# DLRM tower on one core: dense matmuls, stores and the last steps of the tail put in another order

## The reference

```python
e = jnp.stack([tbl_f[ids[:, f]] for f in range(39)], axis=1)      # (512, 39, 16)
xk, outs = e, []
for W in (W0, W1):
    Wr = W.reshape(39, xk.shape[1], 128)
    xk = jnp.einsum('bid,bjd,ijh->bhd', e, xk, Wr)
    outs.append(xk)
z = jnp.sum(jnp.concatenate(outs, axis=1), axis=-1)               # (512, 256)
h = jnp.concatenate([z, dense_ctx], axis=1)                       # (512, 272)
h = jnp.maximum(h @ W_top1 + b_top1, 0.0)                         # (512, 512)
h = jnp.maximum(h @ W_top2 + b_top2, 0.0)                         # (512, 256)
y = h @ W_top3                                                    # (512, 1)
```

## Time and profile before

| what | value |
|---|---|
| median of 3 runs | 257.5 us |
| lowest and highest of them | 256.31 and 258.46 us |
| the profiled execution's own time | 257.7 us |
| its span (first to last instruction) | 255.9 us |
| PE, DVE, POOL, ACT busy | 211.4, 180.1, 157.0, 149.3 us |
| mean granted clock of PE | 0.946 |

### The profile page before, as it was taken

How to read it: one execution, slowest core, us unless ns; L and a number is a source line. 1 busy time by engine, 2 the same in 40 slices (tenths; PEclk the granted TensorE clock), 3 DMA queues, 4 the chain that set the end, 5 groups by cost and what they waited for, 6 DMA issues and landing times.

```text
span 255.9 us, 3948 instructions
## 1 busy us (share of the span) xinstructions
PE 211.4 (83%) x1212; PEld 165.7 (65%) x1212; DVE 180.1 (70%) x335; ACT 149.3 (58%) x284; POOL 157.0 (61%) x165
## 2 busy tenths in 40 slices
PE   0458294971989898999898979997989799998996
PEld 0223153750766586888575868885768688876995
DVE  1497595944899979796979696969796968841000
ACT  2134254670778766776687566776876566866002
POOL 4777777777677777777777777777777750000000
PEclk9999859597699999999999999999999799999799
DMA  6200032295411202020202020202020201010000
GB/s 193 68 6 6 7 52 69 39 280 135 108 20 20 31 10 33 9 33 8 32 9 33 9 31 6 32 9 33 8 32 9 32 9 19 6 27 4 0 3 0
DMA packets 27511, 9.40 MB, mean 37 GB/s; under 512 B 22513, under 2 KB 25585, under 8 KB 27490
## 3 DMA queue, kind: packets, MB, share of 16 engines
q1 hardware_dynamic: 22370, 7.86, 13.7%
q0 software_dynamic: 5120, 1.29, 5.3%
HBM read 6.50 MB, written 0.00 MB: 25 GB/s over the span
## 4 chain that ended last, share of the span: by engine, by line
PE 42%; POOL 26%; issue 12%; DMA 9%; DVE 8%; ACT 2%; DVEq 0%; ACTq 0%; POOLq 0%
POOL gathered L348 26%; PE tower L671 10%; DMA gathered<-table,rows 8%; PE copies L622 7%; PE sums L636 4%; PE sums L637 4%; PE sums L638 4%; PE ring L660 3%; PE ring L661 2%; PE ring L662 2%; DVE turned L408 2%; DVE parts L399 1%; ACT dots L532 1%; DVE columns L442 1%; PE ring L650 1%
## 5 line engine op out<-in xcount | busy, mean ns | idle before, releaser
L348 POOL DMA_INDIRECT gathered<-table,rows x160 | 156.6, 979 | 51.7 <-issue 44.2
L428 DVE TENSOR_TENSOR prod_lo<-prod,prod_hi 128x512 fp32r<-128x512 f32 x96 | 65.0, 690 | 3.3 <-ACT prod_hi L498 3.3
L622 PE MATMUL copies<-turned,sel_sb 128*128 128x512 bf16 x112 | 42.7, 434 | 28.9 <-DVE turned L408 28.6
L420 DVE TENSOR_TENSOR prod<-first,copies 128x512 f32<-128x512 f32 x96 | 64.0, 681 | 2.8 <-ACT first L489 1.3
L498 ACT CAST prod_hi<-prod 128x512 fp32r<-128x512 f32 x96 | 58.2, 625 | 9.1 <-DVE prod L420 9.1
L671 PEld LDWEIGHTS tower<-dots,w_sb 128*128 128x128 f32 x312 | 47.7, 199 | 5.0 <-issue 0.8
L671 PE MATMUL tower<-dots,w_sb 128*128 128x128 f32 x312 | 49.8, 284 | 0.3 <-ACT dots L532 0.2
L532 ACT COPY dots<-ring 128x320 f32<-128x320 f32 x64 | 43.6, 746 | 8.0 <-PE ring L662 6.9
L636 PE MATMUL sums<-prod_hi,w_hi 128*128 128x512 f32 x96 | 47.6, 496 | 0.4 <-DVE prod_lo L428 0.2
L637 PE MATMUL sums<-prod_lo,w_hi 128*128 128x512 f32 x96 | 38.8, 404 | 0.0
L622 PEld LDWEIGHTS copies<-turned,sel_sb 128*128 128x128 bf16 x112 | 10.3, 103 | 44.0 <-DVE turned L408 33.8
(11 more groups left out here) (85 smaller groups left out, 237.8 us busy)
## 6 DMA issues: line engine op xcount, KB each, us to landing
gathered<-table,rows POOLq DMA_INDIRECT x160
diag<-columns SPq DMA_DIRECT2D x128, 20.0 KB
wt_sb<-wt SPq DMA_DIRECT2D x2, 512.0 KB
sel_f<-sel SPq DMA_DIRECT2D x1, 448.0 KB, 3.0
w0a<-w_ij SPq DMA_DIRECT2D x1, 448.0 KB, 4.4
w0b<-w_ji SPq DMA_DIRECT2D x1, 448.0 KB, 5.4
ids_sb<-ids SPq DMA_DIRECT2D x1, 85.0 KB, 2.0
ident_f<-ident SPq DMA_DIRECT2D x1, 64.0 KB, 2.8
```

Of the source, the lines that this page charges most:

```text
L348: pool.indirect_dma_start(gathered[0:n, k % NGATHER, q, :], None, table, bass.IndirectOffsetOnAxis(ap=rows[0:n, k, q:q + 1], axis=0)).then ...
L420: nc.vector.tensor_tensor(prod[:, m % NPROD, :], first[:, k % 2, :], copies[n % 3][:], ALU.mult)\
L428: nc.vector.tensor_tensor(prod_lo[:, m % NPART, :], prod[:, m % NPROD, :], prod_hi[:, m % NPART, :], ALU.subtract).then_inc(lo_ready, 1)
L622: pe.matmul(copies[n % 3][:], sel_sb[:, e, :], turned[:, k % NTURN, :], start=True, stop=True).then_inc(copied, 1)
```

## The change

1. A new step `last_dense` in PE's order, right ahead of `x1` of block 15: the four 16-row matmuls of the dense features of group 3 (what L701 did), one into each h1 bank.
2. Of the last block's four dot stores ACT keeps 0 and 2; DVE takes 1 and 3, after its last low part.
3. Tower step 3 of group 2 (PE's L693) is moved from between the last dots to behind layer 2, and ACT's two relus of step 2 from ahead of the last dot stores to behind them.
4. Layer 2 of group 3 starts right after the last dot stores. Its bank is `sums[1]` in place of `tower`; `tower` becomes the first h2 bank. The four z1 matmuls (what L700 did) and tower step 3 of group 2 follow it.
5. DVE takes two of the four h1 relus (1 and 3).

No DMA is added or moved.

```diff
--- before.py
+++ after.py
@@ -124,8 +124,8 @@
 
 GROUP_TENSOR = (dict(layer2=6.22, rate=2.58, tower=(23.18, 26.7, 31.41)),
                 dict(layer2=6.11, rate=2.84, tower=(24.45, 27.61, 30.02)),
-                dict(layer2=6.49, rate=2.72, tower=(22.71, 30.79, 31.9)))
-GROUP_SCALAR = ((23.33, 26.23, 29.15, 32.32), (22.1, 26.57, 28.3, 32.76), (21.63, 26.88, 32.35, 75.59))
+                dict(layer2=6.49, rate=2.72, tower=(22.71, 30.79)))
+GROUP_SCALAR = ((23.33, 26.23, 29.15, 32.32), (22.1, 26.57, 28.3, 32.76), (21.63, 26.88, 34.6))
 GROUP_VECTOR = (23.59, 23.68, 25.09)
 
 
@@ -140,7 +140,8 @@
                 if isinstance(steps, float):
                     items.append((STEPS * k + steps, (name, k)))
                 else:
-                    items.extend((STEPS * k + step, (name, k, n)) for n, step in enumerate(steps))
+                    items.extend((STEPS * k + step, (name, k, n)) for n, step in enumerate(steps)
+                                 if items is not act or (name, k) != ("dot", BLOCKS - 1) or n % 2 == 0)
     for g in range(GROUPS - 1):
         end = STEPS * (GROUP // BLOCK) * (g + 1)
         when = group_tensor[g]
@@ -148,6 +149,7 @@
         pe.extend((end + step, ("tower", g, n + 1)) for n, step in enumerate(when["tower"]))
         act.extend((end + step, ("tower", g, n)) for n, step in enumerate(group_scalar[g]))
         dve.append((end + group_vector[g], ("h1", g)))
+    pe.append((STEPS * (BLOCKS - 1) + tensor["x1"] - 0.01, ("last_dense",)))
     return [[what for _, what in sorted(items, key=lambda x: x[0])] for items in (pe, act, dve)]
 
 
@@ -224,7 +226,8 @@
         dense_banks = [*sums, tower, sums[0]]
 
         h1_banks = [*copies, sums[0]]
-        h2_banks = [sums[1], ring[0]]
+        z2_bank = sums[1]
+        h2_banks = [tower, ring[0]]
         y_bank = ring[1]
 
 
@@ -269,8 +272,11 @@
         tower_drained = sem("tower_drained")
         h1_summed = sem("h1_summed")
 
+        last_dots = sem("last_dots")
+        last_z2_full = sem("last_z2_full")
+        last_z2 = sem("last_z2")
         last_h1_full = sem("last_h1_full")
-        last_h1 = sem("last_h1")
+        last_h1 = [sem(f"last_h1_{n}") for n in range(H1 // P)]
         last_h2_full = sem("last_h2_full")
         last_h2 = [sem(f"last_h2_{n}") for n in range(H2 // P)]
         last_y_full = sem("last_y_full")
@@ -286,6 +292,13 @@
 
         def by_sub(of):
             return of[:, 0:SUBS * WIDE].rearrange("p (s i) -> p s i", i=WIDE)
+
+        def dots_at(k, s):
+            g, at = divmod(k * BLOCK + s * SUB, GROUP)
+            return dots[:, g % 2, :, at:at + SUB].rearrange("p i b -> p b i")
+
+        def dots_of(n):
+            return ring[n % 2][:, 0:SUB * WIDE].rearrange("p (b i) -> p b i", i=WIDE)
 
         block = ctx.enter_context(nc.Block())
 
@@ -463,7 +476,15 @@
                 {"split": split, "columns": columns_low, "product": product, "low": low,
                  "squares": square_low, "x1": turned_low, "h1": h1_sum}[what[0]](*what[1:])
 
+            for s in range(1, SUBS, 2):
+                n = ring_no["dot", BLOCKS - 1, s]
+                dve.wait_ge(ring_full, n + 1)
+                nc.vector.tensor_copy(dots_at(BLOCKS - 1, s), dots_of(n)).then_inc(last_dots, 1)
             dve.wait_ge(tower_in, 16 * 4)
+            for n in range(1, H1 // P, 2):
+                dve.wait_ge(last_h1_full, n + 1)
+                nc.vector.tensor_scalar(h1[:, n, :], h1_banks[n][:, 0:GROUP], bt1_sb[:, n:n + 1], 0.0,
+                                        ALU.add, ALU.max).then_inc(last_h1[n], 1)
             dve.wait_ge(last_h2_full, 2)
             nc.vector.tensor_scalar(h2[:, 1, :], h2_banks[1][:, 0:GROUP], bt2_sb[:, 1:2], 0.0,
                                     ALU.add, ALU.max).then_inc(last_h2[1], 1)
@@ -529,9 +550,7 @@
                 if g >= 2 and at == 0:
 
                     act.wait_ge(tower_full, NMLP * (g - 2) + 2)
-                nc.scalar.copy(dots[:, g % 2, :, at:at + SUB].rearrange("p i b -> p b i"),
-                               ring[n % 2][:, 0:SUB * WIDE].rearrange("p (b i) -> p b i", i=WIDE))\
-                    .then_inc(ring_drained, 1)
+                nc.scalar.copy(dots_at(k, s), dots_of(n)).then_inc(ring_drained, 1)
 
             def tower_step(g, step):
                 act.wait_ge(tower_full, NMLP * g + step + 1)
@@ -562,11 +581,13 @@
                  "high": high, "squares": square_both, "sums": store_x1, "x1": store_turned,
                  "dot": store_dots, "tower": tower_step}[what[0]](*what[1:])
 
-            tower_step(GROUPS - 1, 0)
-            for n in range(H1 // P):
+            act.wait_ge(last_z2_full, 1)
+            nc.scalar.copy(z2[:], z2_bank[:, 0:GROUP]).then_inc(last_z2, 1)
+            tower_step(GROUPS - 2, 3)
+            for n in range(0, H1 // P, 2):
                 act.wait_ge(last_h1_full, n + 1)
                 nc.scalar.activation(h1[:, n, :], h1_banks[n][:, 0:GROUP], ACT.Relu,
-                                     bias=bt1_sb[:, n:n + 1]).then_inc(last_h1, 1)
+                                     bias=bt1_sb[:, n:n + 1]).then_inc(last_h1[n], 1)
             act.wait_ge(last_h2_full, 1)
             nc.scalar.activation(h2[:, 0, :], h2_banks[0][:, 0:GROUP], ACT.Relu, bias=bt2_sb[:, 0:1]).then_inc(last_h2[0], 1)
             act.wait_ge(last_y_full, 1)
@@ -578,7 +599,9 @@
 
                 if n >= 2:
                     was = ring_order[n - 2]
-                    if was in low_no:
+                    if was == ("dot", BLOCKS - 1, 1):
+                        pe.wait_ge(last_dots, 1)
+                    elif was in low_no:
                         pe.wait_ge(ring_low, low_no[was] + 1)
                     else:
                         pe.wait_ge(ring_drained, n - 1)
@@ -694,42 +717,54 @@
                                        start=(j == 0), stop=(j == H2 // P - 1))
                 mm.then_inc(tower_full, 1)
 
-            def last_first_layer(n):
-
-                to, cols = h1_banks[n][:, 0:GROUP], slice(P * n, P * n + P)
-                pe.matmul(to, wt1_sb[:, 0, cols], dots[:, (GROUPS - 1) % 2, FIELDS, :], start=True, stop=False)
-                pe.matmul(to, wtd_sb[:, cols], dense_t[:, GROUP * (GROUPS - 1):], start=False, stop=False)
+            def last_dense():
+
+                pe.wait_ge(prod_ready, TILES * BLOCKS)
+                pe.wait_ge(first_ready, BLOCKS)
+                pe.wait_ge(sums_stored, BLOCKS - 1)
+                for n in range(H1 // P):
+                    pe.matmul(h1_banks[n][:, 0:GROUP], wtd_sb[:, P * n:P * n + P], dense_t[:, GROUP * (GROUPS - 1):],
+                              start=True, stop=False)
+
+            def last_second_layer(i):
+                mm = pe.matmul(z2_bank[:, 0:GROUP], w1_sb[:, i, :], dots[:, (GROUPS - 1) % 2, i, :],
+                               start=(i == 0), stop=(i == FIELDS - 1))
+                if i == FIELDS - 1:
+                    mm.then_inc(last_z2_full, 1)
 
             turn_dense()
             for what in pe_order:
                 if what[0] in ("first", "second"):
                     copy_rows(what)
+                elif what[0] == "last_dense":
+                    last_dense()
                 else:
                     {"columns": fields_by_column,
                      "tile": add_tile, "sum_squares": add_squares, "x1": turn_x1, "dot": dot,
                      "layer2": second_layer, "tower": tower_step}[what[0]](*what[1:])
 
 
-            pe.wait_ge(prod_ready, TILES * BLOCKS)
-            pe.wait_ge(first_ready, BLOCKS)
             pe.wait_ge(sums_stored, BLOCKS)
-            pe.wait_ge(ring_drained, ring_no["dot", BLOCKS - 1, SUBS - 1] + 1)
-            last_first_layer(0)
-            last_first_layer(1)
+            pe.wait_ge(ring_drained, ring_no["dot", BLOCKS - 1, 1] + 1)
+            pe.wait_ge(last_dots, SUBS // 2)
             for i in range(FIELDS):
-                second_layer(GROUPS - 1, i)
-            last_first_layer(2)
-            last_first_layer(3)
-            pe.wait_ge(tower_drained, NMLP * (GROUPS - 1) + 1)
+                last_second_layer(i)
+            for n in range(H1 // P):
+                pe.matmul(h1_banks[n][:, 0:GROUP], wt1_sb[:, 0, P * n:P * n + P], dots[:, (GROUPS - 1) % 2, FIELDS, :],
+                          start=False, stop=False)
+                if n == 1:
+                    tower_step(GROUPS - 2, 3)
+            pe.wait_ge(last_z2, 1)
             for n in range(H1 // P):
                 pe.matmul(h1_banks[n][:, 0:GROUP], wt1_sb[:, 1, P * n:P * n + P], z2[:],
                           start=False, stop=True).then_inc(last_h1_full, 1)
+            pe.wait_ge(tower_drained, NMLP * (GROUPS - 1))
             for j in range(H1 // P - 1):
-                pe.wait_ge(last_h1, j + 1)
+                pe.wait_ge(last_h1[j], 1)
                 for n in range(H2 // P):
                     pe.matmul(h2_banks[n][:, 0:GROUP], wt2_sb[:, j, P * n:P * n + P], h1[:, j, :],
```

(2 more changed lines are left out.)

## The result

The changed kernel takes 252.91 us (median of four runs, 252.3 to 254.41). The kernel before, over four runs, has 257.98 (256.31 to 259.58). Every run of the changed kernel is shorter than every run of the kernel before. The medians lie 5.1 us apart (0.980). The ratio of the two kernels is given as 0.9874, with a 95% interval of 0.9825 to 0.9924: 3.3 us faster, between 2.0 and 4.5. It does not follow from these eight runs as they stand (their means give 0.981), so the size of the gain in whole time is known only as 2 to 5 us. The forecast was 254.1.

What follows compares the result with a forecast made beforehand. PE was taken to carry the chain of the last 26 us, with a low clock inside layer 2. Terms of -1.89 us at an equal clock and -1.7 for the clock took 257.7 to 254.1; range 253.0 to 256.3.

Steps and rivals of the forecast that it cites:

- (a): Between the last dot stores and layer 2: two pairs of dense and z1 matmuls leave the path, minus 1.64 us.
- (b): Last dot stores: ACT begins earlier and DVE stores beside it, so layer 2 starts earlier, minus 0.36 us.
- (c): Behind layer 2: twelve 128-row passes replace two matmul pairs, minus 0.24 us, and 0.1 more for L725.
- (d): Two h1 relus on DVE near the end: already hidden, so zero; some 0.05 us if the first were late.
- (e): Dense matmuls ahead of the x1 transposes: eight 16-row passes delay the transposes and all behind, plus 0.45 us.
- The second rival: Dense matmuls ahead of x1: 16-row passes keep 0.21 us each, costing 1.05 us; kernel at 254.7; chance 0.13.
- (g): Clock in layer 2: with PE's idle and half-rate stretch ahead of it gone, it stays at 1.00, minus 1.7 us.
- the first rival: Layer 2: no gain from the clock, only the 1.89 us stays; kernel at 255.6; chance 0.33.
- The third rival: Last dot stores: DVE's strided store out of PSUM far dearer than ACT's, deciding from 1.6 us a store; chance 0.03.

Runs made afterwards that it cites:

- Part 1 alone: Kernel before with only the four 16-row dense matmuls moved ahead of the x1 transposes; tail 21.32 us against 23.23, whole-time ratio to before 0.9866.
- part 3 undone: Changed kernel with ACT's group 2 relus ahead of the last dot stores and tower step 3 between dots 1 and 2 again; tail 21.02 us against 21.67.
- parts 1 and 4 undone: Changed kernel with 16-row matmuls again paired with z1 matmuls, two pairs ahead of layer 2, two behind; tail 27.01 us, ratio to before 1.0038.
- the pairs doubled: Kernel before with pairs 2 and 3 of z1 and dense matmuls done once more ahead of layer 2; tail 24.91 us against 23.23, clock 1.00.

## Why the prediction was right, and where it was not

The forecast of 254.1 was 1.2 us above the measured 252.91, which is just under the low end of my range, with the median of before at 257.98 in place of 257.5. I forecast a gain of 3.6 us. The ratio puts it at 3.3, the medians at 5.1, and the tails of the two profiles at 3.2. Of these 3.2 us, 1.56 are what the change does at an equal clock. The other 1.62 are a fall of the clock that this one execution of before had and the next did not. So that the total came near the forecast is in part luck: the profile that I predicted from happened to hold the fall, and the other fall, at 201 us, widened the gap once more for no reason in the change. By the steps of the sum:

(a) The pairs off the path ahead of layer 2: forecast -1.64. Layer 2 follows the last store directly, against the timeline above. Right. Part 1 alone takes the alternating pairs away both ahead of layer 2 and behind it, and gives 1.91 us, more than the whole gain of 1.56 at an equal clock, since part 3 takes 0.65 back.

(b) The stores: forecast -0.36, measured -0.20 (dot 0 to layer 2 went from 5.39 to 3.55 us, and 1.64 of that is (a)). The mis-sized term is DVE's store: 0.70 us in place of 0.60, inside 0.48 to 0.76 and nearer its upper end. DVE pays for the 512-byte step as ACT does. The Trainium skill ("SBUF — State Buffer", the note on cachelines) had that sign; the trace agrees, 0.70 against the 0.48 that I interpolated from the contiguous rows. The other 0.06 is dot 2, which starts 1.56 us behind dot 0 where I had 1.50.

(c) Behind layer 2: forecast -0.34, measured 0. This is the step that failed. From layer 2's end to the first pass of the second dense layer it was 2.56 us (248.57 to 251.13), and is 2.55 (243.86 to 246.41). I took twelve passes at 0.111. The timeline shows 1.61 us for them, 0.28 more. The first pass of 1-column weights starts 0.21 us behind the 128-column one ahead of it (244.19 to 244.40), and the first and second 128-column pass behind those start 0.20 and 0.21 behind their predecessors. I knew this price for the change between 128 and 16 rows, from the earlier trace rows, and did not see that step 3 changes the width. In its old place, in a wait of PE, all this was hidden. Moving it cost 0.65 us (part 3 undone). The rest of (c), the pairs taken apart, did gain.

(d) The relus: 0 forecast, 0.06 measured.

(e) The dense matmuls: +0.45 forecast, +0.35 measured. The second rival, 0.21 for every 16-row pass, was wrong: six passes take 0.93 us, so 0.13 us apart on average ((0.93 - 0.27) / 5), which is one step of 0.21 and four of 0.11. The earlier trace rows led the right way, but my reading of them rested on more than they show. I took their 0.64 us for passes at 1.2 GHz, while the granted clock that the profile gives for 11 to 16 us is 1.00, at which 0.64 would be twice the dense price and would have spoken for the rival. That PE does run at half pace there shows in other rows: two 128-row passes of 512 columns start 0.40 us apart (19.83 and 20.23), and 0.22 in the earlier trace rows.
```profile
19.83 1.04 PE L622 MATMUL copies<-turned,sel_sb 128*128 128x512 bf16 x2 [3.42 <-DVE turned L408]
```
The Trainium skill's rule that weight loads overlap only when the row group differs ("TensorE: Matmul & The Clock Gate", Part 3) does not hold here: passes on the same rows run dense, 0.11 us apart, and it is the change between two heights or widths that costs some 0.1 us at a time.

Sum at an equal clock: -1.89 forecast, -1.56 measured.

(g) The clock: -1.7 forecast, -1.62 between the two profiles (12.00 less 10.38, which is layer 2 to the z2 matmuls in the kernel before without the fall). The size was right. The reason I gave is not shown. Of five profiles with alternating pairs ahead of layer 2 two had the fall (one of two of the kernel before, and the one with parts 1 and 4 undone), of nine without such pairs none. That points the way of the theory, but with so few it can be chance, and the profile with the pairs doubled, where the theory demanded the fall, did not have it. At 200 us, an idle time of 2.06 us was followed by a fall and one of 2.00 us was not. What makes the fall come in one execution and not in another stays open. So the first rival holds in part: an execution of before may have no fall, and the change is then worth 1.6 us. On the first chip the medians differ by more. The clock row shows a further difference between the two profiles, the fall at 201 us, in work that the change does not touch. How often the unprofiled runs had either fall is not known.

The third rival, a DVE store of 1.6 us or more, was wrong: 0.70.

## What to carry to other kernels

Group matmuls by the shape of their weights. Alternating 128-row and 16-row (or 128-column and 1-column) float32 passes cost here 0.21 us a pass against 0.11, and a pass of another shape belongs into a wait of PE rather than into a dense stretch. When a step is moved out of a wait, ask what hid it there: tower step 3 was all but free between the dots (part 3 undone starts layer 2 0.07 us later) and cost 0.65 us behind layer 2. And before a low-clock stretch is booked as a gain, profile a second execution of the same kernel: one profile shows its size, not how often it comes.

## What the runs showed of the hardware that was not expected

A change of the weights' width costs PE much what a change of their height does: 0.28 us for going from 128 columns to 1 and back, in steps of 0.1 us on the passes at and behind the change. The weight loads show what differs. The load of the first pass of a new shape starts together with the pass (both at 228.23 for the first dense pass of the changed kernel), while within one shape the load starts 0.11 us ahead of its pass (228.45 and 228.56 for the third). DVE and ACT store a 128x320 tile out of PSUM with a 512-byte step in the same 0.70 us, though contiguous tiles of 512 columns take DVE 0.68 and ACT 0.58. The same program took 50 us more on two other chips. In the profile of it from one of them PE, DVE and ACT stand still together for some 3 us at a time while only POOL works (104 to 107 us), with DVE waiting up to 3.8 us for nothing that the profile names. Yet the tail up to layer 2 was the same there to 0.01 us (8.65 in both). And at the start of the span PE ran at about half pace (0.40 against 0.22 us a pass) while the profile gave its granted clock as 1.00.
